# Vision transformer tower: gate scores from raw tokens, causal mask by TensorE, attention scores of the second half ahead of the output step of the first

## What is computed

```python
h = h + _L1_attn_ref(_layernorm(h), ...)   # 16 heads, rank-64 scores, causal over the 6 tokens
h = h + _L1_ffn_ref(_layernorm(h), ...)    # 8 experts

# in _L1_attn_ref
att = jnp.einsum('bhts,bus->bhtu', lt, latent) * (1.0 / math.sqrt(R))
att = jnp.where(causal[None, None], att, jnp.float32(-jnp.inf))
att = jax.nn.softmax(att, axis=-1)
...
y = y @ o_w.T + o_b

# in _L1_ffn_ref; x is the layer-normalised h
scores = (jnp.tanh(xf @ gate_w.T) + 1.0) * 0.5
vals, idx = jax.lax.top_k(scores.T, k)               # k = 48 of 384 tokens for each expert
y = _layernorm(xf[flat_idx].reshape(k, n, d), ln_gamma, ln_beta)   # a second layer norm
h = gelu(einsum(y, fc1s) + b1s); o = einsum(h, fc2s) + b2s
out = xf.at[flat_idx].add(o * kept_w)
```

## Time and profile before

| | |
|---|---|
| time, median of 3 runs (lowest, highest) | 234.01 us (233.98, 235.32) |
| the profiled execution: its own time | 233.83 us |
| its span, first to last instruction | 232.0 us |
| mean granted TensorE clock | 0.991 |
| busy: PE, PEld | 218.9 us (94%), 174.7 us (75%) |
| busy: DVE, ACT, POOL | 136.5 us (59%), 71.2 us (31%), 59.7 us (26%) |
| chain that ended last, by engine | PE 79%, DVE 14%, issue 3%, ACT 2%, POOL 1% |
| warming matmuls, L431 | 33.4 us busy in 124 records |

### The profile page before, as it was taken

The page is one execution under the profiler, slowest core; times in us unless marked ns, Lnnn a source line. Parts: engine busy times, 40 slices in busy tenths (PEclk is TensorE's granted clock), DMA queues, the critical chain, the costliest instruction groups (busy, mean ns, idle before and its releaser), DMA issues.

```text
span 232.0 us, 3985 instructions
## 1 busy us (share of the span) xinstructions
PE 218.9 (94%) x1442; PEld 174.7 (75%) x1442; DVE 136.5 (59%) x424; ACT 71.2 (31%) x178; POOL 59.7 (26%) x118
## 2 busy tenths in 40 slices
PE   8999999999969999999999999999979899999995
PEld 6888888889958787779678877887758664655673
DVE  2697567576567565568567558668669525231212
ACT  2124232185667445214223320223030043130310
POOL 1044562366521132030241411221085140000000
PEclk9999999999999999999999999999999889999999
DMA  6999446930000000059999980000002205783002
GB/s 175 349 349 394 175 111 178 440 161 1 3 0 1 3 0 3 0 186 418 429 262 349 429 370 4 3 0 1 3 1 69 68 3 131 318 350 107 0 0 68
DMA packets 9747, 34.31 MB, mean 148 GB/s; under 512 B 1280, under 2 KB 3840, under 8 KB 7424
## 3 DMA queue, kind: packets, MB, share of 16 engines
q1 hardware_dynamic: 9728, 34.07, 40.8%
HBM read 32.88 MB, written 0.39 MB: 143 GB/s over the span
## 4 chain that ended last, share of the span: by engine, by line
PE 79%; DVE 14%; issue 3%; ACT 2%; POOL 1%; DVEq 0%; POOLq 0%
PE bank L442 18%; PE bank L999 6%; PE bank L973 6%; PE bank L664 5%; PE bank L566 4%; PE bank L673 4%; PE bank L544 3%; PE bank L591 3%; PE bank L431 3%; PE bank L941 3%; PE bank L725 2%; PE bank L736 2%; PE bank L454 2%; PE bank L1006 2%; PE bank L467 2%
## 5 line engine op out<-in xcount | busy, mean ns | idle before, releaser
L442 PE MATMUL bank<-desk,bench 118*126 118x256 f32 x190 | 43.7, 383 | 0.0
L442 PEld LDWEIGHTS bank<-desk,bench 118*126 118x126 f32 x190 | 35.5, 191 | 5.0
L431 PE MATMUL bank<-zeros 128*128 128x256 f32 x124 | 33.4, 405 | 1.1 <-POOL small L1932 1.1
L1937 POOL TENSOR_TENSOR small<-small 96x2 f32<-96x2 f32 (+2 forms) x15 | 9.9, 662 | 67.1 <-DVE small L1269 48.7
L431 PEld LDWEIGHTS bank<-zeros 128*128 128x128 f32 x124 | 23.1, 199 | 4.5 <-POOL small L1932 1.1
L1697 ACT ACTIVATE attic<-bank,cols 128x126 f32<-128x126 f32 x38 | 15.2, 452 | 14.0 <-PE bank L454 13.9
L1053 DVE TENSOR_REDUCE bench<-bench 118x70 f32<-118x630 f32 x19 | 14.7, 798 | 5.8 <-DMA bench<-patches 5.8
L1690 ACT ACTIVATE desk<-bank 126x256 f32<-126x256 f32 x19 | 7.3, 382 | 25.1 <-PE bank L442 21.9
L1945 POOL TENSOR_TENSOR small<-small 126x1 f32<-126x1 f32 x19 | 10.5, 565 | 16.3 <-DVE small L1059 11.4
L664 PE MATMUL bank<-bench,layw 128*128 128x192 f32 x72 | 13.1, 331 | 0.5 <-ACT bench L1753 0.4
L664 PEld LDWEIGHTS bank<-bench,layw 128*128 128x128 f32 x72 | 11.6, 190 | 1.5 <-ACT bench L1753 1.3
(11 more groups left out here) (197 smaller groups left out, 408.6 us busy)
## 6 DMA issues: line engine op xcount, KB each, us to landing
attic<-experts SPq DMA_DIRECT2D x10, 1024.0 KB, 8.7
desk<-experts SPq DMA_DIRECT2D x6, 1024.0 KB, 17.4
bench<-patches SPq DMA_DIRECT2D x19, 315.0 KB, 4.5
desk<-tokenizer_w SPq DMA_DIRECT2D x4, 576.0 KB, 5.8
layw<-layer_w SPq DMA_DIRECT2D x1, 2184.0 KB, 11.5
attic<-bias SPq DMA_DIRECT2D x8, 256.0 KB, 11.9
cons<-constants SPq DMA_DIRECT2D x1, 1258.0 KB, 5.6
desk<-conv_w SPq DMA_DIRECT2D x5, 128.0 KB, 3.4
```

The lines of the kernel that those rows point to most:

```text
L431: mm(bank[b][:, 0:C], zeros[:, 0:P], zeros[:, :], start=True, stop=True)
L442: i = mm(conv_bank[t % 2][0:TP, 0:C], xt[t % XRING][0:KP, k, :], convw[0:KP, k, :], start=(k == 0), stop=(k == KX - 1))
L1937: pool.tensor_tensor(rs, var, half[0:parts, 0:rs.shape[1]], ALU.pow).then_inc(s(name), 1)
```

## The change

Seven edits, one after another in the code:

1. `ternary_mean` (PE) and `ternary_scale` (DVE), near 104 us: two more matmuls of 8 columns give the channel mean of the gate weights, and two more DVE operations give `gate_w`, the gate weights less that mean. With centred weights, the mean of a token's channels drops out of its score, so gate scores can be taken from raw `h`.
2. The end of the last residual: `norm(3, g)` and `turn_x(3, g)` are gone. `turn_h(g)` turns `h` itself once it is added. `gate_scores` puts tokens on the partitions (eight matmuls of 8 columns in all), ACT's tanh multiplies by the token's inverse root as its scale, two activations for each half, and `turn_gate` turns the result back to experts by tokens; `halve` reads it from PSUM.
3. `att_mask(g)` on PE writes the mask into the bank by one matmul of 384 columns with the identity as weights, and `att_scores` adds on top. `att_shift` on DVE loses the addition and reads PSUM in its two remaining operations.
4. PE's list: `att_mask(1)` and `att_scores(1)` stand before `latent_out(0)`; the whole gate stands behind `latent_out(1)`.
5. DVE's list: `add_mixed(0)` moves from before `att_shift(1)` to behind the last `sum_keys(1, 5)`; `norm(3, g)` and `twice_normed(g)` are gone.
6. The second layer norm: statistics of `xn` are replaced by a formula. POOL's `shift_again(g)` makes scale and shift in five dependent small operations, and `norm_again` moves to ACT, four activations on `h`. `xh2` takes the place of `xn` in memory.
7. Warming matmuls: before `att_scores(0)` 1 for 3; after the second half's scores 3 for the 5 + 1 that were there; before `latent_out(1)` 2 for 3; behind it 1, 1 and 1 between the gate's steps for 7 + 1.

```diff
@@ PE
+                for k in range(KC):
+                    i = mm(bank[0][:, E8:2 * E8], mean_m, lw["gate"][:, k, :], start=(k == 0), stop=(k == KC - 1))
+                i.then_inc(s("w_mean_done"), 1)
...
+            def att_mask(g):
+                pe.wait_ge(s("lt_dve"), 2 * g + 1)
+                mm(bank[4 * g][0:AR, 0:2 * GT].rearrange("q (i n) -> q i n", n=4 * T), ident[0:AR, 0:AR],
+                   causal.unsqueeze(1).to_broadcast([AR, GI // 2, 4 * T]), start=True, stop=False, skip_group_check=True)
...
+            def turn_h(g):
+                pe.wait_ge(s(f"h_ready{g}"), 3)
+                for u in range(TG):
+                    for k in range(KC):
+                        i = pe.transpose(bank[4 * g + 1][:, k * GT + u * TR:k * GT + (u + 1) * TR],
+                                         h[0:TR, TG * g + u, k * P:(k + 1) * P], ident[0:TR, 0:TR])
+                i.then_inc(s(f"x_turned{g}"), 1)
...
             def gate_scores(g):
+                pe.wait_ge(s("w_chain"), 5)
                 pe.wait_ge(s(f"xT_ready{g}"), 4)
-                for k in range(KC):
-                    i = mm(bank[4 * g + 2][0:E8, 0:GT], lw["gate"][:, k, :], xT[:, g, k, :],
-                           start=(k == 0), stop=(k == KC - 1))
+                for u in range(TG):
+                    for k in range(KC):
+                        i = mm(bank[4 * g + 2][0:TR, u * E8:(u + 1) * E8], xT[:, g, k, u * TR:(u + 1) * TR],
+                               gate_w[:, k, :], start=(k == 0), stop=(k == KC - 1))
                 i.then_inc(s("gate_done"), 1)
+
+            def turn_gate(g):
+                pe.wait_ge(s("gate_tanh2"), TG * (g + 1))
+                for u in range(TG):
+                    i = pe.transpose(bank[4 * g + 2][0:E8, P + u * TR:P + (u + 1) * TR],
+                                     gate_tok[0:TR, TG * g + u, :], ident[0:TR, 0:TR])
+                i.then_inc(s(f"x_turned{g}"), 1)
...
@@ DVE
-                dve.wait_ge(s("w_mean_done"), 1)
+                dve.wait_ge(s("w_mean_done"), 2)
...
+                ts(gate_mean, bank[0][:, E8:2 * E8], float(C), None, ALU.mult).then_inc(s("w_chain"), 1)
+                dve.wait_ge(s("w_chain"), 4)
+                tt(gate_w, lw["gate"], gate_mean.unsqueeze(1).to_broadcast([P, KC, E8]), ALU.subtract)\
+                    .then_inc(s("w_chain"), 1)
...
             def att_shift(g):
+                scored = bank[4 * g][0:AR, 0:2 * GT].rearrange("q (i t) -> q i t", t=T)
                 dve.wait_ge(s("att_scored"), g + 1)
-                flat_a = att[0][g].rearrange("q i b p t -> q i (b p t)")
-                tt(flat_a, a4(bank[4 * g][0:AR, 0:2 * GT]),
-                   causal.unsqueeze(1).to_broadcast([AR, GI // 2, 4 * T]), ALU.add).then_inc(s("att_chain"), 1)
...
+                dve.tensor_reduce(st(0, g), scored, AX.X, ALU.max).then_inc(s("att_chain"), 1)
+                dve.wait_ge(s("att_chain"), 2 * g + 1)
+                tt(a3(1, g), scored, bc(st(0, g)), ALU.subtract).then_inc(s("att_chain"), 1)
...
             heads_out(1)
-            add_mixed(0)
             att_shift(1)
-            norm(3, 0)
             att_norm(1)
-            twice_normed(0)
...
             sum_keys(1, 5)
+            add_mixed(0)
+            add_mixed(1)
             halve(0)
-            add_mixed(1)
-            norm(3, 1)
-            twice_normed(1)
             halve(1)
...
@@ ACT
             def gate_out(g):
                 act.wait_ge(s("gate_done"), g + 1)
+                act.wait_ge(s(f"t_rs_ready{g}"), 4)
+                for u in range(TG):
+                    t = TG * g + u
+                    ac(gate_tok[0:TR, t, :], bank[4 * g + 2][0:TR, u * E8:(u + 1) * E8], ACT.Tanh,
+                       scale=t_rs[0:TR, t:t + 1]).then_inc(s("gate_tanh2"), 1)
+
+            def norm_again(g):
+                act.wait_ge(s("again"), 5 * (g + 1))
+                for t in range(TG * g, TG * (g + 1)):
+                    ac(xh2[0:TR, t, :], h[0:TR, t, :], ACT.Identity, bias=t_d2[0:TR, t:t + 1],
+                       scale=t_s2[0:TR, t:t + 1]).then_inc(s("xh2_ready"), 1)
...
             xT_out(3, 0)
+            xT_out(3, 1)
+            gate_out(0)
+            gate_out(1)
+            norm_again(0)
+            norm_again(1)
             with_norm(1, 0)
-            gate_out(0)
-            xT_out(3, 1)
-            gate_out(1)
             with_norm(1, 1)
             act.wait_ge(s("vals_turned"), 1)
...
@@ POOL
+            def shift_again(g):
+                sl = slice(TG * g, TG * (g + 1))
+                pool.tensor_tensor(t_sq[0:TR, sl], t_rs[0:TR, sl], t_rs[0:TR, sl], ALU.mult).then_inc(s("again"), 1)
+                pool.wait_ge(s("again"), 5 * g + 1)
+                pool.tensor_scalar(t_again[0:TR, sl], t_sq[0:TR, sl], -EPS, 1.0 + EPS, ALU.mult, ALU.add)\
+                    .then_inc(s("again"), 1)
+                pool.wait_ge(s("again"), 5 * g + 2)
+                rsqrt(t_again[0:TR, sl], t_sq[0:TR, sl], "again", parts=TR)
+                pool.wait_ge(s("again"), 5 * g + 3)
+                pool.tensor_tensor(t_s2[0:TR, sl], t_rs[0:TR, sl], t_sq[0:TR, sl], ALU.mult).then_inc(s("again"), 1)
+                pool.wait_ge(s("again"), 5 * g + 4)
+                pool.tensor_tensor(t_d2[0:TR, sl], t_nm[0:TR, sl], t_s2[0:TR, sl], ALU.mult)\
+                    .then_inc(s("again"), 1)
...
+            rs_tokens(3, 0)
+            rs_tokens(3, 1)
             rs_and_shift(3, 0, 1)
-            rs_tokens(4, 0)
             rs_and_shift(3, 1, 1)
-            norm_again(0)
-            rs_tokens(4, 1)
-            norm_again(1)
```

More of the change, by code:

```diff
@@ L725, in att_scores @@
                     i = mm(bank[4 * g][0:AR, im * 2 * T:(im + 2) * 2 * T],
-                           ltT[g][:, im * T:(im + 2) * T, :], latD[g][:, im:im + 2, :, :], start=True, stop=True)
+                           ltT[g][:, im * T:(im + 2) * T, :], latD[g][:, im:im + 2, :, :], start=False, stop=True,
+                           skip_group_check=True)
                 i.then_inc(s("att_scored"), 1)
@@ L897, in _ @@
             head_products(1)
+            keep_warm(0, 1)
+            att_mask(1)
+            att_scores(1)
             latent_out(0)
-            att_scores(1)
-            keep_warm(3, 5)
-            turn_x(3, 0)
-            keep_warm(3, 1)
-            gate_scores(0)
+            keep_warm(3, 3)
             spread_att(1, 0)
@@ L909, in _ @@
             spread_att(1, 5)
-            keep_warm(3, 3)
+            keep_warm(3, 2)
             latent_out(1)
-            keep_warm(3, 7)
-            turn_x(3, 1)
+            turn_h(0)
             keep_warm(3, 1)
+            turn_h(1)
+            gate_scores(0)
             gate_scores(1)
+            turn_gate(0)
+            keep_warm(3, 1)
+            turn_gate(1)
+            keep_warm(3, 1)
             pe.wait_ge(s("halved"), G)
@@ L1391, in halve @@
             def halve(g):
-                dve.wait_ge(s("gate_tanh2"), g + 1)
-                sl = slice(g * GT, (g + 1) * GT)
-                ts(val8[:, sl], work8[0][:, sl], 1.0, 0.5, ALU.add, ALU.mult).then_inc(s("halved"), 1)
-            def twice_normed(g):
-                dve.wait_ge(s(f"xn_ready{g}"), 4 * TG)
-                norm_stats(4, g, xn)
+                dve.wait_ge(s(f"x_turned{g}"), 5)
+                ts(val8[:, g * GT:(g + 1) * GT], bank[4 * g + 2][0:E8, P:P + GT], 1.0, 0.5, ALU.add, ALU.mult)\
+                    .then_inc(s("halved"), 1)
             window_sums(0)
@@ L2028, in rs_and_shift @@
                     .then_inc(s("shift_ready"), 1)
-            def norm_again(g):
-                pool.wait_ge(s(f"t_rs_ready{g}"), 5)
-                for n in groups:
-                    pool.wait_ge(s(f"h_ready{n}"), 3)
-                for t in range(TG * g, TG * (g + 1)):
-                    pool.tensor_scalar(xh2[0:TR, t, :], xn[0:TR, t, :], t_mv[0:TR, t, 0:1], t_rs[0:TR, t:t + 1],
-                                       ALU.subtract, ALU.mult).then_inc(s("xh2_ready"), 1)
             def bias_base(g):
```

26 lines of the change are left out of this document (11 added, 15 removed).

## The result

| | before | after |
|---|---|---|
| time, median of 4 runs (lowest, highest) | 234.0 us (232.56, 235.32) | 231.1 us (231.04, 231.22) |
| ratio, 95% interval | | 0.9884 [0.9844, 0.9923] |
| span of the profiled execution | 232.0 us | 229.3 us |
| warming matmuls (L431, now L433), records | 124 | 104 |

A forecast was written before the change was run, and what follows sets the result against it. The prediction took a relay of short steps from 137 to 181 us, with five waits touching the change, as the bound. Its terms summed to -3.2 us, taken as -3.1, giving 230.9 us, range 229.2 to 232.6.

The forecast's parts named there:

- (a) to (d): Waits at the first half's softmax, second half's scores, second softmax to spread, and last output step to search (6.01 us).
- signs of being wrong: PE's clock falling before search, marks' turn waiting for PE, `valT` or moves releasing next step, DVE PSUM operations over 0.6 us.
- Gate weights' mean: Near 104 us: two more matmuls of 8 columns behind the mean matmul, on the chain, cost +0.3 us.
- Mask in the first half: First half's softmax: DVE loses 0.59 us, of which 0.35 is gained, as PE idled only 0.35 before the spread.
- Second half's scores earlier: Second half's scores start at about 152.6 in place of 153.09, with ACT's copy last: -0.5 us.
- Mask and gate out of the way: Second half, softmax to spread: mask saves 0.59 us on DVE, the 0.33 before the spread falls to 0.04; -0.9.
- The tail: Last output step to first search round: 4.25 us in place of 6.01; gain 1.76, between 1.2 and 2.1.
- What follows the search: Search to gather: no wait; warming matmuls have 0.1 us to spare, `valT` just in time, moves 0.7 to spare.
- the search would hold POOL's small steps up: Rule cited under rival of late moves: POOL's small operations lose search steps, gather 1 to 3 us late; rival's chance 0.1.
- The clock: Rivals: low clock in the tail, 232 to 233 us, chance 0.12; dip in the gather gone, 229.2, chance 0.12.

## Why the prediction was right, point by point

The forecast was 230.9 us, 3.1 under the median of before; measured are 231.1 and 2.9. The mechanism held: the waits (a) to (d) became shorter in the way that the prediction says, and none of its signs of being wrong appeared. That the number is this close is in part luck. The terms missed by 0.16, 0.18, 0.25 and 0.12 us, in both directions.

*Gate weights' mean.* Forecast +0.3, measured +0.46. The rate of the score matmuls, 0.17 us each, was too low a price: these took 0.23 each. Their weights have 128 columns for the scores' 96; whether that is the reason is not shown. The direction (nothing hides them) was right, and the kernel with the mean moved takes them off the chain.

*Mask in the first half.* Forecast -0.35; measured -0.68 + 0.15 = -0.53. The mask matmul took 0.89 us behind a wait, not 0.67, and the scores start 0.1 us later after DVE's first copy. But the 0.35 us of idle before the spread was not all the room that PE had, so nearly all of DVE's 0.59 counted. PE's timeline after shows why:

```profile
141.12 1.03 PE L433 MATMUL bank<-zeros 128*128 128x256 f32 x4
141.98 1.52 PE L748 MATMUL bank<-bench,cons 96*128 96x32 f32 x12
```

The spread's first record begins 0.17 us before the end of the warming matmuls ahead of it (141.12 + 1.03 = 142.15). An idle time is counted from such a modelled end, so the room was 0.35 + 0.17 = 0.52 us.

*Second half's scores earlier.* Head products to scores fell by 0.49, forecast 0.5, and ACT's copy was what came last (151.14 + 1.57 = 152.71, scores at 152.76 in the chain). Half of it, 0.24, came back at once: the scores took 2.91 us on the chain in place of 2.67. It is the same overlap: the 153.09 of before was the modelled end of the output step; on PE's timeline the first score matmul's own record begins at 152.92. A start read from a chain between two PE groups is late by such an overlap, and this term was sized 0.24 too large. (The output step ahead took 1.90 us on the chain of before, not the 1.98 of the last one, which changes nothing, as ACT came last.)

*Mask and gate out of the way.* Forecast -0.88, measured -0.87, and the spread starts 0.04 us behind DVE's last product, as forecast. Order and mask needed each other here: alone, the mask gained nothing, since PE's list stood behind DVE.

*The tail.* Forecast 4.25 us, measured 4.13: the gate matmuls took 1.43 us in all, the pair of tanh 0.42 (0.35 was assumed), `halve` 0.36 from PSUM (0.26 was assumed), and hand-overs made up for it. This is the largest piece, 1.88 us. The kernel with order and mask alone isolates it: its tail is 6.10 us against 4.13, so the raw gate is worth 1.97 less the 0.46 that its mean costs, 1.5 us; the times at full clock (230.85 less 229.4 to 229.6) say 1.2 to 1.5. There is a little more to be had: ACT ends the last tanh at 169.22 + 0.42 = 169.64, but `turn_gate(1)` starts on the chain at 169.82, behind a warming matmul (L433 at 169.36), so up to 0.18 us of the tail is the kernel's own warming.

*What follows the search.* Forecast: no wait, 0.1, 0.1 and 0.7 us to spare. The warming matmuls ended at 170.74 + 6.74 = 177.48 by PE's timeline, 0.3 us before the search did:

```profile
170.74 6.74 PE L433 MATMUL bank<-zeros 128*128 128x256 f32 x30
```

`valT` was there at 176.80, 1 us before the marks' turn began; the normalised tokens had landed by 178.13, 1.9 us before the gather. POOL was overpriced: a dependent step under the search took 0.27 us, not 0.37 to 0.44 (170.55 to 170.82), so the last product came 7.3 us after the last output step, not 8.7. The prediction feared that the search would hold POOL's small steps up, by the rule of the Trainium skill (SBUF — State Buffer, "SBUF: two separate sides") that a DVE instruction with two SBUF inputs locks GpSimd's reads out. Most of the search can't show it: MAX8 (L1638) names one tile as input, and the steps at 170.55 and 170.82 lie under it. MATCH_REPLACE8 names two, on DVE's timeline:

```profile
171.10 0.53 DVE L1641 MATCH_REPLACE8 bench<-small,bench 8x384 f32<-8x384 f32 x1
```

Under it POOL's step at 171.29 took 0.19 us as well. So nothing of the rule shows here; whether this instruction counts as one with two SBUF inputs, no run shows.

*The clock.* The forecast kept the fall in the gather, and each of the four runs had a mean granted clock of 0.993, the profiled one with its single fall there. That all four had this fall and no other is luck too: three of the ten later runs of this kernel, at 0.978, read 232.69 to 232.87 us, over the upper end of the range, and the prediction had no term for a fall near 100 or 141 us. In the tail the clock stayed at 1.00 with twelve transposes in it, in all eight traces of kernels that have this tail. By the rule on transposes in the Trainium skill (TensorE: Matmul & The Clock Gate, Part 4: PE-mode transpose) it should rather have fallen; these traces don't agree with it, without refuting it.

What stays open: why the clock falls in one execution and not in the next, and whether warming before the gather prevents it.

## What to carry to other kernels

In a relay of short steps across engines, count what stands between two fixed points and remove whole hand-overs: taking the normalisation behind the matmul, as a scale of the activation and a centred weight, took three steps out of nine, put one in, and took 1.9 us off the tail. An operation saved on one engine counts only if the next engine's list is free at that moment: the mask alone gained nothing, the order alone 0.4 us, both 1.5 by the traces. A matmul behind running work costs less than behind a wait, here by 0.2 us or so; an idle time or a start read next to a PE group is off by as much. Before a difference of 1% is believed, compare executions at the same granted clock, and then the stretches of their traces.

## What was not expected of the hardware

PE's granted clock fell to 1.2 GHz in different places of one kernel from one execution to the next: in the changed kernel in the gather alone, or near 96 and 141 us and not in the gather. The places seen are near 69 to 72, 96 to 104, 136 to 144, 164 to 170 and 180 to 188 us over all kernels traced here. The kernel before alone had means from 1.000 down to 0.962 and times from 232.4 to 238.5 us. What makes it fall in one execution and not in the next, the traces don't show. The same gather took 5.85 us with a fall in it and 4.17 without. One matmul of 384 columns with a 96 x 96 identity took 0.89 us on the chain behind a wait and 0.65 right behind an output step; the second is near its columns' share, 0.67, of a warming one in a row (0.45 for 256).
